# The first loads of an attention and router kernel: who issues them, who rounds them, and two fewer warm-up products

## The reference

```python
x = x + xattn(layernorm(x), ctx, ctx, pos, mask, Wq, Wk, Wv, Wo)
x = x + ffn(layernorm(x), router_weight, router_bias, expert_bias)
# xattn: q = x Wq, k = ctx Wk, v = ctx Wv; rotary embedding of q and k;
#        softmax(q k^T / sqrt(128), masked) v, then Wo
# ffn:   softmax(x router^T + bias), the 8 largest kept: x * sum(kept) + kept @ expert_bias
```

## Time and profile before

| what | value |
|---|---|
| median of 3 runs | 586.71 us (586.17 to 586.82) |
| the profiled execution, its own time | 589.14 us |
| its span, first to last instruction | 587.0 us |
| first real product of TensorE | 6.95 us |
| last of the 48 first products starts | 19.31 us |

### The profile page before, as it was taken

How to read it: one execution, slowest core, us unless ns; L and a number is a source line. 1 busy time by engine, 2 the same in 40 slices (tenths; PEclk the granted TensorE clock), 3 DMA queues, 4 the chain that set the end, 5 groups by cost and what they waited for, 6 DMA issues and landing times.

```text
span 587.0 us, 10608 instructions
## 1 busy us (share of the span) xinstructions
PE 578.1 (98%) x2999; PEld 490.4 (84%) x2999; DVE 471.9 (80%) x763; ACT 401.2 (68%) x1066; POOL 434.1 (74%) x407
## 2 busy tenths in 40 slices
PE   8999999998999999999999999999999999999997
PEld 7888888887888888888888888888888888888885
DVE  5669797798888788877977798779877986797987
ACT  5257754786777777777776777677776776586655
POOL 5468599699977787687868886888678865446554
PEclk9999999999999999999999999999999999999999
DMA  8953526111411310131012111311121012100002
GB/s 284 375 164 109 156 89 217 52 36 47 136 35 55 90 54 20 55 89 54 18 54 89 54 32 39 89 54 54 28 79 57 14 47 62 36 20 2 19 37 91
DMA packets 30960, 45.39 MB, mean 77 GB/s; under 512 B 3024, under 2 KB 11600, under 8 KB 30928
## 3 DMA queue, kind: packets, MB, share of 16 engines
q1 hardware_dynamic: 30256, 43.82, 23.4%
q0 software_dynamic: 384, 1.05, 0.5%
q10 hardware_dynamic: 288, 0.14, 0.1%
HBM read 35.03 MB, written 9.96 MB: 77 GB/s over the span
## 4 chain that ended last, share of the span: by engine, by line
PE 89%; DVE 4%; POOL 3%; issue 2%; ACT 1%; DMA 1%; SPq 0%; DVEq 0%; ACTq 0%
PE score L1863 9%; PE outp L1887 8%; PE outp L1891 8%; PE outp L1895 8%; PE bank_a L1737 4%; PE probT L1942 4%; PE bank_a L1735 4%; PE bank_a L1736 4%; PE attnT L1721 2%; PE attnT L1723 2%; PE attnT L1722 2%; PE bank_c L1735 2%; PE bank_c L1737 2%; PE bank_c L1736 2%; POOL wo_lo L547 1%
## 5 line engine op out<-in xcount | busy, mean ns | idle before, releaser
L542 POOL TENSOR_TENSOR rot<-rot,sinT 128x512 f32<-128x512 f32 x75 | 103.4, 1380 | 43.2 <-ACT rot L830 43.1
L1005 ACT ACTIVATE probs<-score,negmax 128x128 f32<-128x128 f32 x256 | 90.7, 366 | 27.8 <-DVE negmax L1398 27.8
L660 POOL TENSOR_TENSOR probs<-probs,rsum 128x512 f32<-128x512 f32 x64 | 69.4, 1084 | 44.1 <-DVE rsum L1404 44.1
L1887 PE MATMUL outp<-wo_hi,oT_hi 128*128 128x512 f32 x240 | 94.7, 396 | 0.0
L1891 PE MATMUL outp<-wo_lo,oT_hi 128*128 128x512 f32 x240 | 93.4, 391 | 0.3 <-POOL wo_lo L547 0.3
L1895 PE MATMUL outp<-wo_hi,oT_lo 128*128 128x512 f32 x240 | 83.4, 389 | 0.0
L1411 DVE TENSOR_TENSOR resid<-resid,outp 128x512 f32<-128x512 f32 x60 | 41.0, 683 | 48.8 <-PE outp L1895 46.9
L1863 PEld LDWEIGHTS score<-kT,qT 128*128 128x128 f32 x512 | 66.9, 191 | 4.9
L1240 DVE TENSOR_TENSOR qT<-qT,rot 128x512 f32<-128x512 f32 x57 | 68.2, 1199 | 2.9 <-POOL rot L542 0.5
L1014 ACT ACTIVATE pT_hi<-probT 128x512 fp32r<-128x512 f32 x64 | 38.4, 600 | 43.0 <-PE probT L1942 42.5
L1863 PE MATMUL score<-kT,qT 128*128 128x128 f32 x512 | 67.4, 274 | 0.0
(11 more groups left out here) (364 smaller groups left out, 1531.6 us busy)
## 6 DMA issues: line engine op xcount, KB each, us to landing
ring_b<-in_wo SPq DMA_DIRECT2D x32, 256.0 KB, 2.9
ring_a<-in_wq SPq DMA_DIRECT2D x28, 256.0 KB, 2.8
v_dram<-v_stage SPq DMA_DIRECT2D x16, 256.0 KB, 4.2
v_raw<-v_dram SPq DMA_DIRECT2D x16, 256.0 KB, 2.6
k_dram<-k_stage SPq DMA_DIRECT2D x14, 256.0 KB, 2.1
kT<-k_dram SPq DMA_DIRECT2D x14, 256.0 KB, 2.8
ctx_in<-in_ctx SPq DMA_DIRECT2D x8, 256.0 KB, 6.3
ring_b<-in_wv SPq DMA_DIRECT2D x8, 256.0 KB, 8.2
```

Of the source, the lines that this page charges most:

```text
L542: pool.tensor_tensor(rot_of(k0), rot_of(k0), sinT[:, half * W:(half + 1) * W], ALU.mult).then_inc(sin_done, 1)
L660: pool.tensor_tensor(probs[:, p], probs[:, p], rsum[:, p, :].unsqueeze(2).broadcast_to([P, GH, S]), ALU.mult).then_inc(soft_done, 1)
L1005: last = act.activation(probs[:, p, h, :], heads(score[p][:, :])[:, h, :], ACT.Exp, bias=negmax[:, p, h:h + 1], accum_out=sums[:, p, h:h + 1])
L1887: pe.matmul(ps[:, :], oT_hi[:, cols], wo_hi[:, h, :], start=h == 0, stop=False)
```

## The change

- The first context chunk (half 0, c = 0) is issued by ScalarE, as its first instruction, ahead of `pos`. SyncE's list therefore begins with weights 0, and every transfer behind it stands one place further forward.
- The rounding copies of the four context chunks of half 0 move from ScalarE to VectorE. The first one stands ahead of the three small operations on `pos`, the others ahead of the subtraction of their chunk. ScalarE's list has the four weight copies in a row, and then waits for `ctx_hi` to reach 4 before it rounds the second half of the context (so that the count tells which chunks are there).
- `WARM` goes from 10 to 8.

```diff
-WARM = 10
+WARM = 8
@@ sync
             for c in range(C):
-                load_ctx(0, c)
+                if c:
+                    load_ctx(0, c)
                 load_wv(c)
@@ scalar
+            act.dma_start(ctx_in[:, 0, 0:W], ctx[0:P, 0:W]).then_inc(dma_ctx[0], 16)
             act.dma_start(pos_in[:, :], pos).then_inc(dma_pos, 16)
...
             for c in range(C):
-                hi_ctx(0, c)
                 hi_wv(c)
+
+            act.wait_ge(ctx_hi, C)
             for c in range(C):
                 hi_ctx(1, c)
@@ vector
             dve.memset(rot[:, 0, :], 0.0).then_inc(warm_done, 1)
+
+            def hi_ctx(c):
+                dve.wait_ge(dma_ctx[c], 16)
+                dve.tensor_copy(ctxT_hi[:, c, 0:W], ctx_in[:, c, 0:W]).then_inc(ctx_hi, 1)
+
+            hi_ctx(0)
             dve.wait_ge(dma_pos, 16)
...
             for c in range(C):
+                if c:
+                    hi_ctx(c)
                 lo_ctx(0, c)
```

## The result

The changed kernel takes 588.34 us (median of 7 executions, 587.50 to 589.24), the kernel before, run beside it, 586.82 us (7, 586.17 to 587.10). The ratio is 1.0027, with a 95% interval of 1.0018 to 1.0037: slower by a quarter of a per cent, where 585.0 us had been forecast.

The account below looks back on a forecast made before the run. TensorE, busy 98% of the span, was taken as the bound. Starting its products 1.75 us earlier, with the other parts hidden or put at 0, gave 586.71 - 1.75 = 584.96 us, ratio 0.997; range 583.9 to 587.2 us.

Parts of the forecast that it names:

- the 1.75 us: At TensorE's start: real products begin at about 5.2 us instead of 6.95, and everything behind moves 1.75 us earlier.
- the prediction's last sentence: If undisturbed runs lack the slow transfer stretch, before starts right behind the unread products at 6.1 us; gain 0.9 us.
- the 1 us to spare: Second chunk's data: ready at 8.5 us, TensorE asks at about 9.5 us, so hidden with 1 us to spare.
- The transfers at 3.8 us: First context and weights, issued in parallel at about 0.73 us, land at about 3.8 us; the other end was 5.7.
- only the issue time is saved: Rival, 20%: weights land at 5.7 us, first product at 6.5 us, a gain of 0.45 us, 586.26 us.
- One more issue ... costs nothing: ScalarE's added issue of about 0.4 us ahead of its table load lies ahead of any landing and costs nothing.
- The unread products: TensorE's warm-up: four rows fewer end 0.93 us earlier, at 5.16 us; operands rounded by 4.45, real products from about 5.2.
- As long after the first real product: TensorE's clock rises 3.4 us after the first real product, as before, so the gain is the whole 1.75 us.
- the rival of the same instant: Rival, 14%: the clock rises at the same instant as before, leaving 0.93 us of the gain, 585.8 us.
- The rival of the early rise: Rival, 12%: unread products count, the clock rises 1 to 3.4 us earlier relative to the first product; gain 2.6, 584.1 us.
- The slower rival: Rival, 8%: weights or context land after 6 us, TensorE idles 1.8 us, clock rises later; 587.9 us, 588.4 at worst.
- the rival in which VectorE becomes the bound: Rival, 4%: copies take 1.2 us, a chunk 2.6 us on VectorE; about 1 us of gain is left, 585.7 us.

Follow-up runs that it names:

- before with eight: The kernel before with 8 unread products (WARM) instead of 10, nothing else changed: 586.69 us, ratio 1.0002.
- the transfers alone: The kernel before with the first context issued by ScalarE ahead of pos, rounding left on ScalarE, WARM 10: 587.72 us, ratio 1.0019.
- the transfers taken back: The changed kernel with the transfers issued as before; VectorE rounds, WARM 8: 586.38 us, ratio 0.9996 to before.
- The kernel in which SyncE waits: The changed kernel with WARM 10, SyncE waiting for both first transfers to land before issuing the next ones: 590.61 us, ratio 1.0057 to before.
- before with four: The kernel before with 4 unread products (WARM) instead of 10: 588.19 us, ratio 1.0023.
- After with the positions behind and eight products: The changed kernel, WARM 8, with VectorE's three operations on pos put behind its first two subtractions: 586.74 us, ratio 1.0009 to before.
- after with the issues exchanged: The changed kernel with ScalarE's two issues swapped, pos first, then context 0: 589.09 us, ratio 1.0039 to before.
- its repetition: The changed kernel, unchanged, profiled and timed once more: 587.55 us, ratio 1.0019 to before.
- after with 10: The changed kernel with 10 unread products (WARM) instead of 8: 587.46 us, ratio 1.0011 to before.
- with 12: The changed kernel with 12 unread products (WARM) instead of 8: 587.61 us, ratio 1.0015 to before.
- positions behind with 10: The changed kernel with WARM 10 and VectorE's three operations on pos behind its first two subtractions: 586.48 us, ratio 0.9998 to before.
- before again: The kernel before, unchanged, profiled and timed once more: 586.70 us, ratio 1.0008.
- only the rounding: The kernel before with the first half of the context rounded by VectorE, transfers as before, WARM 10: 586.75 us, ratio 0.9996.
- weights first: The kernel before with the first weights ahead of the first context, both on SyncE's queue: 586.74 us, ratio 0.9998.

## Why the prediction was wrong, point by point

**The sum's base.** The step that failed first is the 1.75 us itself: it was read from an execution 2.4 us above the median, and then taken from the median. "The same difference gives 586.71 - 1.75" treats the 2.4 us as lying elsewhere, but they lie where the gain was sought. In the usual execution that was profiled the weights are rounded from 4.11 us, the first product follows the unread ones at 5.69 us (not at 6.1, as the prediction's last sentence had it), and the clock has risen. Fewer unread products could let it start earlier, but the second chunk was not ready before about 8.5 us there, and that is when TensorE came to it: the 1 us to spare that the prediction found there was the lower level of the clock. The last sentence of the prediction named this case, but with the wrong reason and a gain of 0.9 us: the slow stretch is there in a usual execution too (57 GB/s at the lowest in the second profile of before). What sets the rare execution apart is the late rise of the clock. Weights that land late are not rare by themselves: they did so in three of the six profiles with that order of transfers, and one of the three, before with eight, took 587.00 us.

**The transfers at 3.8 us.** Failed. "No byte of the two needs to move after 3.5 us" supposed that the first 516 KB belong to the first two transfers. With two queues they do not: the next transfers of SyncE's queue and the positions share the DMA engines. By 5.75 us the seven profiles with the context first on ScalarE's queue, without the wait, had moved 948 to 1010 KB, the seven with both on SyncE's queue 778 to 895 KB; by 3.5 us it was 379 to 479 against 463 to 522 KB. More was moved in all, but not for the two that were waited for: they landed at 4.6 to 5.9 us in the profiles with the moved transfers (5.07 and 5.24 us in after). With both on one queue, context first, the context landed at 3.4 to 3.8 us, and the weights by 4.1 to 4.6 us in three profiles and at 5.6 to 6.2 us in three others. Held alone, the two landed at 4.2 and 4.4 us. The rival that only the issue time is saved, 6.5 us for the first product, was too low a gain against the profile of before and too high against a usual execution: in the medians even the 0.46 us of issue did not come through. The Trainium skill, "DMA: Bandwidth & Descriptors", section "Issuing engines are not separate DMA queues", says that issues on several engines save only the sequencer's time. The medians agree and lie below that bound: no kernel with the moved transfers is faster than before by more than its interval. The two profiles of before and after can't test it: the weights landed 1.08 us earlier in after, but the landing differs by 2 us among profiles with one and the same order of transfers.

**"One more issue ... costs nothing".** Failed, and this is the whole loss in the executions of the low kind. The step looked at ScalarE's own work and not at the transfer behind the moved one. The positions left 0.45 us later but landed 2.7 us later, at 6.3 us: 5.1 us from issue to landing where it had been 2.9. The prediction had the row numbers 0.7 us later and asked who needs them; it was right that nobody does. It missed who stands behind them: VectorE runs its list in order, and the first low context and first low weights are behind the three position operations. The low context was begun at 6.8 to 7.3 us instead of 4.1 us, and used at 7.7 to 8.05 us, in every profile with the moved transfers and the positions in front, except where SyncE waited. Three comparisons show it: the transfers alone cost 1.03 us, the transfers taken back give it back, and with the operations moved behind, the transfers stay and the loss goes (0.77 us above before, then 0.18 below). The kernel in which SyncE waits adds the cause of the late landing: there the positions took 3.4 us instead of 5.1, so it is not the place behind the context alone, but SyncE's next transfers beside it (one profile).

**The unread products.** Their length was right (0.237 us for a row of the timeline, end at 5.24 us for 5.16 forecast). But the forecast needed the operands at 4.45 us. With the weights usable only at 5.7 us TensorE idles 0.63 us.

**The clock.** "As long after the first real product" failed: it was 4.6 us in after, 3.4 us in the profile of before and 5.7 us in before with four, and in the remaining thirteen profiles the clock rises at 4.4 to 7.4 us, in nine of them ahead of the first real product. Between the two profiles of before and after the rival of the same instant has the right sum: 1.08 us earlier at the lower level, 0.51 us of it left at the fifth value product; the other profiles show that there is no such fixed instant. The unread products do count, other than "4.64 us of unread products did not raise the clock before" had it. The rival of the early rise was right in its mechanism and wrong on who profits: before already had it.

The slower rival's 587.9 to 588.4 us holds the measured 588.34, but by luck: its condition (the weights land after 6 us) did not come, and in the low kind of execution, nine of the eighteen of after, the loss is that of the positions, of which it says nothing. One part of its mechanism did come in the profile of after: an idle stretch ahead of the first product at the lower level, and a rise at 10.4 us. Such a stretch isn't enough, though. After with the positions behind and eight products idled 0.82 us, and after with the issues exchanged 1.51 us, both behind unread products made wholly at the lower level (3.78 us for sixteen rows, as in after), and the clock was up at their first real product.

The profile of after lies 0.97 us above that of its repetition, in which the clock rose early, and the high single times lie 1.0 to 2.2 us above the middle of the others. How often a time was above 588.2 us:

| transfers | unread products | above 588.2 us | kernels |
|---|---|---|---|
| moved | 8 | 13 of 30 | after (5 of 7), its repetition (4 of 11), positions behind (4 of 12) |
| moved, issues exchanged | 8 | 4 of 5 | positions first |
| moved | 10 or 12 | 1 of 44 | after with 10 and with 12, only the transfers, positions behind with 10 |
| as before | 8 | 2 of 23 | before with 8, transfers taken back |
| as before, weights ahead in one | 10 | 2 of 33 | before again, only the rounding, weights first |
| as before | 10 | 0 of 115 | before beside the four groups |
| as before | 4 | 3 of 7 | before with 4; its fastest time is 587.63 us |

The kernel in which SyncE waits, with all five times above, is left out, since it loses its time elsewhere. So the high times are frequent with the moved transfers and eight unread products together, and rare with either alone. That they come from idle time at the lower level, and that each high time was a late rise, is inferred, since only three profiles are of such executions without another cause (before, after, and before with four); all three show it. What decides between an early and a late rise in one execution is open.

**VectorE's copy, the later chunks, further on.** This part was right for the profile of after. The copy takes 0.43 us, within 0.27 to 0.69 and under the 0.6 us taken. No wait of TensorE for a later chunk appeared in the profile of after, nor one near 34 us, and the last column of the table shows that nothing behind 20 us moved. The spare time ahead of the second chunk, however, is there only while the clock is low: with the transfers taken back TensorE waited 0.47 us for it. The rounding alone has a ratio of 0.9996 [0.9987, 1.0005]; the rival in which VectorE becomes the bound is out.

**The sizes together.** After is 1.5 us slower than before beside it in its first seven executions, and 0.6 us in its repetition (587.55 against 586.99 us). In an execution of the low kind the positions cost 0.7 to 1.0 us, and that is all. In one of the high kind they cost 0.6 us at most, and the rest comes with the late rise. The median hides that there are two kinds: with five of seven high it falls among the high ones, with four of eleven among the low ones. Of the versions tried none beats before by more than the measurement can tell; the nearest is after with the transfers of before, at 0.28 us less, inside its interval.

**Open.** Why the DMA engines are slow from about 3.3 to 5.7 us is not settled. How slow they get depends on the issues: the slowest slice from 3 to 6 us has 49 to 82 GB/s in the seven profiles with both first transfers on SyncE's queue, and 124 to 205 GB/s in the seven with the context first on ScalarE's. They do not lack work there. The row of before with their busy share in tenths has nine tenths at 4.0 to 5.0 us, where they moved 90 to 147 GB/s:

```profile
DMA  0000000469999993999977489999999999999999
```

Nor is it known what lets the first weights land at 4.1 us in one execution of before and at 6.15 us in another. And how SyncE's next transfers hold up the second transfer of ScalarE's queue more than the first was not taken apart.

## What to carry to other kernels

Before a gain is read off one profiled execution, compare its own time with the median: if it lies above, what is about to be removed may be the very thing that made it unusual. A median is worth reading together with the single times, since it can jump between two kinds of execution. When a transfer is put ahead of another on a queue, follow the one behind it through to its reader, and from there through the reader's list, since an engine that works in order hands the wait to everything that stands behind. Where unread products bridge the time to the first operands, cutting them to the usual landing was harmless with the old transfers (2 of 23 high) and not with the later ones (13 of 30): so they are to be measured against the latest landing.

## What the runs showed of the hardware

- A transfer of a few KB, second on ScalarE's queue behind one of 256 KB, needed 5.0 to 5.6 us from issue to landing while SyncE's queue was busy, 3.4 us while SyncE waited (one profile), and 2.9 to 3.2 us as the first on ScalarE's queue.
- Two transfers of 256 KB started at 0.73 us on two queues moved 379 to 479 KB by 3.5 us with all that followed them (seven profiles); on one queue, one after the other, it was 463 to 522 KB (seven). By 5.75 us it was the other way round, 948 to 1010 against 778 to 895 KB.
- TensorE's clock rose during the unread products in seven profiles, at 4.4 to about 6.2 us, and stayed up over 1.1 to 1.2 us of idle time behind them in three. Behind an idle stretch of 2.30 us it fell to 0.51 for about 3.3 us, in the middle of a busy stage. Behind 3.34 us of idle time at the start it rose only at 12.5 us.
- VectorE copies 128x512 from float32 to fp32r in 0.43 us, where its subtraction of the same shape takes 0.69 us and ScalarE's copy 0.63 us.
